# VectorE instead of GpSimd widens the reciprocals of the softmax sums

## The reference

```python
attn = jax.nn.softmax(scores, axis=-1)
out = jnp.einsum('bhcqk,bhckd->bhcqd', attn, vcat)
```

## Time and profile before

| | before |
|---|---|
| median of 3 runs | 3150.91 us (3148.77 to 3153.44) |
| the profiled execution | 3158.34 us |
| its span, first to last instruction | 3156.5 us |
| mean granted TensorE clock | 0.948 |
| PE busy | 2776.2 us |
| DVE busy | 2502.5 us |
| ACT busy | 2397.7 us |
| POOL busy | 2640.5 us, 1590 instructions |
| instructions, all engines | 54604 |

### The profile page before, as it was taken

How to read it: one execution, slowest core, us unless ns; L and a number is a source line. 1 busy time by engine, 2 the same in 40 slices (tenths; PEclk the granted TensorE clock), 3 DMA queues, 4 the chain that set the end, 5 groups by cost and what they waited for, 6 DMA issues and landing times.

```text
span 3156.5 us, 54604 instructions
## 1 busy us (share of the span) xinstructions
PE 2776.2 (88%) x17328; PEld 1765.1 (56%) x17328; DVE 2502.5 (79%) x5644; ACT 2397.7 (76%) x5299; POOL 2640.5 (84%) x1590
## 2 busy tenths in 40 slices
PE   4788788899999999999899899999999899978657
PEld 3555445465565656566565656656565655654326
DVE  3256988889797978889797988979788897989970
ACT  4677878888796978878797888879798787965432
POOL 1116999999998999999999999999899989988870
PEclk9899999999999999999999999999999999999778
DMA  3005353545445454644545464544646454465541
GB/s 84 14 11 168 124 170 98 194 146 186 146 147 195 142 195 144 220 136 138 179 155 192 129 228 144 158 160 145 209 126 214 142 180 152 147 195 189 175 125 42
DMA packets 285967, 477.31 MB, mean 151 GB/s; under 512 B 38451, under 2 KB 93363, under 8 KB 285683
## 3 DMA queue, kind: packets, MB, share of 16 engines
q1 hardware_dynamic: 285682, 473.83, 46.0%
HBM read 388.79 MB, written 84.93 MB: 150 GB/s over the span
## 4 chain that ended last, share of the span: by engine, by line
PE 59%; POOL 17%; DVE 9%; issue 8%; ACT 5%; DMA 1%; SPq 1%; DVEq 0%; POOLq 0%; ACTq 0%
PE bank L765 19%; PE bank L773 8%; POOL h_rows L1786 8%; POOL h_rows L1796 7%; PE bank L1024 6%; PE bank L1010 6%; PE bank L963 5%; PE bank L810 4%; PE bank L888 3%; PE bank L798 3%; PE bank L826 3%; DVE h_rows L1562 2%; PE bank L759 2%; DVE prob L1345 2%; ACT prob L1079 1%
## 5 line engine op out<-in xcount | busy, mean ns | idle before, releaser
L1786 POOL TENSOR_TENSOR h_rows<-u_rows,b_rows 128x1024 f32<-128x1024 f32 x512 | 1203.4, 2370 | 23.2 <-DMA b_rows<-bc_dram 19.4
L1796 POOL TENSOR_TENSOR h_rows<-h_rows,c_rows 128x1024 f32<-128x1024 f32 x480 | 1128.5, 2366 | 76.3 <-DVE state L1569 47.0
L1250 ACT ACTIVATE bank<-d_rows,a_rep 128x512 f32<-128x512 f32 x1024 | 682.2, 689 | 222.6 <-DVE v_pad L1372 82.7
L1562 DVE TENSOR_TENSOR_SCAN h_rows<-bank,state,h_rows 128x512 f32<-128x512 f32 x480 | 593.7, 1269 | 47.6 <-ACT bank L1250 42.5
L1562 DVE TENSOR_TENSOR_SCAN h_rows<-bank,h_rows 128x512 f32<-128x512 f32 x480 | 573.0, 1212 | 63.2 <-ACT bank L1250 46.5
L1079 ACT ACTIVATE prob<-prob,neg_max 128x256 f32<-128x256 f32 x1024 | 510.2, 505 | 36.0 <-DVE neg_max L1345 35.9
L1345 DVE CUSTOM_DVE_ANT_0 prob<-bank,bands 128x256 f32<-128x256 f32 x896 | 336.6, 419 | 122.0 <-PE bank L798 75.4
L810 PE MATMUL bank<-ident,prob 128*128 128x128 f32 x2048 | 330.8, 287 | 87.7 <-ACT prob L1079 55.0
L810 PEld LDWEIGHTS bank<-ident,prob 128*128 128x128 f32 x2048 | 237.5, 144 | 273.4 <-issue 140.3
L963 PE MATMUL bank<-h_rows,sum_n 128*32 128x512 f32 x2048 | 298.0, 662 | 74.3 <-POOL h_rows L1796 55.9
L1010 PE MATMUL bank<-y4T,w 128*128 128x256 f32 x1024 | 250.9, 392 | 12.7 <-DMA e_b<-in_b 10.8
(11 more groups left out here) (164 smaller groups left out, 4852.9 us busy)
## 6 DMA issues: line engine op xcount, KB each, us to landing
u_rows<-u_dram SPq DMA_DIRECT2D x256, 256.0 KB, 3.9
d_rows<-delta_dram SPq DMA_DIRECT2D x256, 256.0 KB, 4.1
b_rows<-bc_dram SPq DMA_DIRECT2D x256, 256.0 KB, 3.1
c_rows<-bc_dram SPq DMA_DIRECT2D x256, 256.0 KB, 3.2
w<-in_W SPq DMA_DIRECT2D x28, 1024.0 KB, 6.8
zs_dram<-region_b SPq DMA_DIRECT2D x64, 256.0 KB, 3.7
xc_dram<-region_b SPq DMA_DIRECT2D x64, 256.0 KB, 2.7
u_dram<-region_b SPq DMA_DIRECT2D x64, 256.0 KB, 5.0
```

The source lines that it names most:

```text
L1250: e.activation(banks[at.bank][:, :], d_rows[:, c, :], ACT.Exp, scale=a_rep[:, k:k + 1]).then_inc(filled[at.bank], 1)
L1562: e.tensor_tensor_scan(rows, banks[at.bank][:, :], rows, start, ALU.mult, ALU.add).then_inc(drained[at.bank], 1)
L1786: e.tensor_tensor(half_of(i, b, half), u_rows[:, 2 * half:2 * half + 2, :], twice(b_rows[:, b % 2, :]), ALU.mult).then_inc(bx_ready.sem, 1)
L1796: e.tensor_tensor(rows, rows, twice(c_rows[:, b % 2, :]), ALU.mult).then_inc(hc_ready.sem, 1)
```

## The change

`widen` moves, word for word, from GpSimd's part of the attention to VectorE's, at the same beat (8w + 11) of the same stage, behind `reciprocals` of the beat before. All numbers of `PLACES`, `THREADS` and `LEADS` are replaced too.

The order that the new numbers give is close to the old one, and not the same. Leaving out `widen` and the empty pieces, VectorE has 2528 pieces; 1897 of their 2527 pairs of neighbours stay neighbours, and no piece moves by more than 8 places. On TensorE it is 1596 of 1831 pairs and 4 places, on ScalarE 1884 of 2878 and 13, on SP's queue 705 of 956 and 8, on GpSimd (with the old place of `widen` kept in the count) 1103 of 1431 and 4. Nearly all of it is one piece of a scan changing places with one piece of another stage beside it. The numbers of the banks differ for most tiles, as they are handed out along the way. The list of ScalarE's functions has 81 changes of table before and after.

On VectorE, `widen` stands right behind `reciprocals` in the windows 1, 3, 4, 5 and 6 of a group in the even part. In the windows 0, 2 and 7 one to three pieces of other stages stand between them (scans, and pieces of the rwkv and middle stages).

```diff
@@ PLACES, THREADS, LEADS: every number replaced, as here
     "attention": (
-        1154, 1246, 1506, 1592, 1696, 1696, 1985, 1985, 2053, 2179, 2244, 2252, 2406, 2454, 2475, 2486, 2495, 2496,
+        1168, 1225, 1458, 1685, 1760, 1920, 2146, 2146, 2146, 2213, 2246, 2246, 2399, 2466, 2481, 2554, 2554, 2554,
...
@@ dve_attention
                     e.wait_ge(*rden_wide_ready.at(i, w - 1))
                 e.reciprocal(rden[:, heads], den[:, c % 2, heads]).then_inc(rden_ready.sem, 1)
 
+            def widen(w):
+                k = w % 2
+                e.wait_ge(*rden_ready.at(i, w + 1))
+                if w > 1:
+                    e.wait_ge(*full(use(f"a{w - 2}")))
+                e.tensor_copy(rden_wide[:, k * P:(k + 1) * P].rearrange("p (h d) -> p h d", d=HD),
+                              rden[:, 8 * k:8 * k + 8].rearrange("p (h o) -> p h o", o=1).broadcast_to([P, 8, HD])
+                              ).then_inc(rden_wide_ready.sem, 1)
+
...
                 if beat % 8 == 2 and beat >= 10 and beat < 72:
                     reciprocals((beat - 10) // 8)
+                if beat % 8 == 3 and beat >= 11:
+                    widen((beat - 11) // 8)
                 yield
@@ pool_attention
-            def widen(w):
-                k = w % 2
-                e.wait_ge(*rden_ready.at(i, w + 1))
-                if w > 1:
-                    e.wait_ge(*full(use(f"a{w - 2}")))
-                e.tensor_copy(rden_wide[:, k * P:(k + 1) * P].rearrange("p (h d) -> p h d", d=HD),
-                              rden[:, 8 * k:8 * k + 8].rearrange("p (h o) -> p h o", o=1).broadcast_to([P, 8, HD])
-                              ).then_inc(rden_wide_ready.sem, 1)
-
...
             for beat in range(AFTER - ATT0):
-                if beat % 8 == 3 and beat >= 11:
-                    widen((beat - 11) // 8)
                 if beat % 8 == 7 and beat >= 15:
```

More of the change, by code:

```diff
@@ L51 @@
     "head": (
-        -1295, -228, -174, 428, 922, 922,
+        -1622, -446, -340, 345, 925, 1156,
     ),
     "attention": (
[6 rows of a table removed]
[6 rows of a table added]
     ),
     "mlp": (
-        8488, 9615, 10328, 10408, 10582, 10582, 10679, 10679, 10862, 10863, 10931, 11191, 11195, 11370, 11370, 11427,
-        11754, 12216, 12231, 12421, 12563, 12813, 12894, 12941, 13050, 13050, 13254, 13314, 13400, 13617,
+        7523, 9595, 10531, 10585, 10622, 10630, 10636, 10636, 10809, 10954, 10954, 11035, 11076, 11264, 11328, 11519,
+        11933, 12203, 12256, 12400, 12610, 12843, 12945, 12995, 13097, 13097, 13294, 13314, 13577, 13617,
     ),
     "rwkv": (
-        14273, 14533, 14534, 14534, 14630, 14717, 14961, 15098, 15171, 15422, 15422, 15496, 15696, 15946, 15978,
-        16191, 16232, 16438, 16546, 16684,
+        14227, 14502, 14503, 14526, 14598, 14667, 14961, 15024, 15189, 15422, 15422, 15528, 15658, 15966, 15997,
+        16227, 16251, 16539, 16539, 16690,
     ),
     "middle": (
-        16764, 16935, 17333, 17392, 17511, 17571, 17650, 17824, 18009, 18084, 18109, 18270, 18298, 18339, 18339,
-        18437, 18459, 18771, 18772, 18772, 18820, 18855, 19035, 19035, 19114, 19608, 19859, 19924, 19936,
+        16792, 16922, 17251, 17377, 17511, 17571, 17650, 17825, 18007, 18064, 18097, 18298, 18298, 18298, 18313,
+        18413, 18516, 18771, 18772, 18878, 18878, 19027, 19176, 19253, 19294, 19843, 19844, 19864, 19990,
     ),
     "scan": (
[10 rows of a table removed]
[10 rows of a table added]
     ),
     "back": (
-        30607, 31803, 31982, 32248, 32346, 32497, 32584, 32830, 33037, 33300,
+        30341, 31789, 31790, 32271, 32380, 32587, 32746, 32833, 33038, 33298,
     ),
     "route": (
-        33454, 33801, 33972,
+        33403, 33805, 33885,
     ),
     "fetch": (
-        43666,
+        43460,
     ),
     "expert": (
-        44497, 44581, 45065, 45317, 45317, 45705, 45845, 46037, 46078, 46628, 46723, 46881, 47060, 47556, 47655,
-        47943, 47960, 48079, 48238, 48825, 48926, 49093, 49247, 49247, 49733,
+        44480, 44590, 45030, 45294, 45294, 45677, 45838, 46035, 46171, 46702, 46718, 46855, 47034, 47521, 47655,
+        47899, 47946, 48074, 48082, 48771, 48885, 49013, 49241, 49241, 49852,
     ),
@@ L103 @@
 THREADS = (
[L104 to L110, removed]
+    (("head", "attention",), (-3974, -1637, -1878, -1870, -1843, -1868, -1867, -1885, -1885, -1885, -1880, -1894, -1879, -1910, -1895, -1945)),
+    (("mlp", "rwkv", "middle",), (-1651, -1880, -1865, -1845, -1870, -1870, -1894, -1887, -1887, -1881, -1881, -1896, -1894, -1889, -1938, -2018)),
+    (("scan",), (-1895, -1834, -1840, -1862, -1868, -1872, -1863, -1885, -1885, -1873, -1870, -1900, -1887, -1923, -1988, -1472)),
+    (("back",), (-1837, -2394, -2397, -1869, -1867, -1832, -1866, -2324, -1884, -1879, -1813, -1858, -2062, -2104, -1875, 313)),
+    (("route",), (1155, -1746, -4346, -1889, -3024, -1590, -1913, -2076, -1979, -1976, -2720, -1774, -1790, -1961, 1979, -289)),
+    (("fetch",), (-2607, -2351, -2014, -2042, -1482, -1852, -2404, -1657, -929, -1904, -1933, -1440, -2236, 713, 997, 5025)),
+    (("expert",), (-1821, -1853, -1867, -1875, -1873, -1873, -1941, -1876, -1884, -1885, -1889, -1952, -2008, -3026, 6197, 8482)),
 )
@@ L117 @@
         "head": (
-            -19, 0, 108, 317, 21, 121,
+            72, 476, 86, 107, -128, -292,
         ),
         "attention": (
[4 rows of a table removed]
[4 rows of a table added]
         ),
         "mlp": (
-            -361, -32, -368, -463, -298, -66, -66, -129, -273, -481, 0, 0, 0, 0, 186, -93, -1, 205, -34, -614, -731,
-            0, -4, -99, -4, -191, 0, 63, -25, -184,
+            -191, -32, -273, -380, -495, -51, -25, 61, -220, -8, 252, -212, 165, -147, 202, -87, -25, 148, 144, -677,
+            -1170, -59, -251, -136, -184, -125, 174, 522, 538, -59,
         ),
         "rwkv": (
-            -4, -31, 235, 169, -539, 233, 0, 29, 55, -126, -27, -425, -23, 0, -684, -333, -358, -493, -358, -358,
+            -1, 42, -59, 40, -83, -89, 7, 74, -93, 0, 0, -38, -38, -38, 0, -80, -88, -49, -2, 0,
         ),
         "middle": (
-            -24, -24, -103, 161, -84, -679, 27, -164, -148, -66, -18, -352, -31, -49, -244, 69, -205, -186, -218, 0,
-            -473, -435, 68, -162, -153, -187, -76, -114, -658,
+            8, -259, -95, 122, -77, -515, 27, -304, -191, -252, -61, -268, 0, -399, -157, 48, -79, -224, -391, -360,
+            -678, -714, 11, -259, -29, -253, 97, -167, -301,
         ),
         "scan": (
[7 rows of a table removed]
[7 rows of a table added]
         ),
         "back": (
-            -1056, 83, -46, -1, -62, 118, -89, -262, 149, 211,
+            -550, 86, 76, -13, 253, -244, -64, -251, 99, 437,
         ),
         "route": (
-            355, -227, -66,
+            -28, 5, 27,
         ),
         "fetch": (
-            -473,
+            -255,
         ),
         "expert": (
-            0, 22, -14, -198, 0, -602, -4, 139, 74, -6, -75, 0, 0, 0, 0, 0, 0, 71, -81, 102, 131, -595, 3, 0, 0,
+            0, 158, 0, -233, 21, -625, -4, 403, -152, 58, 54, 0, 0, 0, 0, 0, 0, -317, -460, 125, 41, 457, 211, 226,
+            0,
         ),
@@ L160 @@
         "head": (
-            20, 74, 215, 285, 51, 51,
+            217, 430, 576, 0, 0, 0,
         ),
         "attention": (
[5 rows of a table removed]
[5 rows of a table added]
         ),
         "mlp": (
-            621, 381, -184, 187, -467, -365, -890, -900, -688, -592, -451, -129, -156, 0, -68, 0, 228, 248, 248, 248,
-            0, 0, 0, 0, -7, 0, 16, 0, 0, 543,
+            234, 232, -263, 0, -285, -169, -9, 188, -77, -526, 0, 0, 0, 0, 0, 210, 0, 0, 0, 0, 0, 0, 0, 0, 0, 0, 0,
+            0, -327, 493,
         ),
         "rwkv": (
-            -101, -155, -26, -176, 18, -235, -42, -42, 0, 379, 571, 314, 14, -74, 6, -44, -1, -19, -207, 0,
+            151, -63, 14, -169, 0, -279, -167, -331, 44, 266, 15, 192, 66, 15, -41, 0, 80, -356, -220, 38,
         ),
         "middle": (
-            0, 279, 0, 0, 84, 172, 0, -41, -133, -599, 14, 80, 0, 0, -125, -177, 82, -48, 75, -121, 180, -17, 352, 0,
-            -346, -808, 260, -445, 0,
+            167, 412, -27, 116, 84, 172, 70, 0, -133, 0, 14, 57, -22, -149, -22, -280, 4, -51, 67, -66, -8, 0, 183,
+            42, -955, -901, 258, 0, 0,
         ),
         "scan": (
[7 rows of a table removed]
[7 rows of a table added]
         ),
         "back": (
-            -76, 232, -106, 30, 18, -1020, 139, 170, 170, 68,
+            -295, 166, -133, -210, 11, -1368, -11, 624, 800, -590,
         ),
         "route": (
-            0, -187, 0,
+            178, 136, -448,
         ),
         "fetch": (
-            174,
+            834,
         ),
         "expert": (
-            -199, -276, 0, 0, 0, -44, -283, 91, 104, 91, -307, -27, -160, 11, 41, -47, -695, -18, -210, -210, 110,
-            67, 93, 299, 909,
+            577, 141, -2, -332, -659, 322, 717, 341, -9, 23, 1, 24, 0, -61, 696, 595, 335, 0, 611, -167, 94, 212, 96,
+            300, -438,
         ),
@@ L205 @@
```

(64 more changed lines are left out.)

## The result

The changed kernel takes 3285.85 us (median of 4 runs, 3283.39 to 3295.55) against 3152.18 for the kernel before on the same chip. The ratio is 1.0425, with a 95% interval of 1.0404 to 1.0445. That is 134 us slower, where 58 were forecast, and above the end of the range, 3272. The profiled execution took 3295.55 us.

The account below looks back on a forecast made before the run. No engine alone was the bound: TensorE, GpSimd and VectorE are full together in the attention windows. Relief 0, copies' wait +58, reordering 0 gave +58 us on 3150.91, so 3209 us, range 3157 to 3240 (0.54); if slower, 3165 to 3272.

Parts of the forecast that it names:

- The size of the copies: 128 copies on VectorE: 0.23 us alone, 1.25 with the wait for GpSimd's multiplications, 130 us in 13 groups.
- The choice between the two rows: VectorE's copy waits for GpSimd like the router's tensor_scalar (2277 ns once), not like the reciprocals (never above 203 ns).
- How much reaches the end: Share of VectorE's added 130 us that reaches the kernel's end: 45%, the middle of two bounds, so 58 us.
- Rival C: All of VectorE's delay is passed on: 73%, 95 us, or 115 with a worse order; 3246 to 3266; chance 0.22.
- The lower bound: In the attention windows VectorE's 7.27 us of idle time absorbs all but 1.48 of 8.75 us of copies: 17%.
- GpSimd's relief: Copies leaving GpSimd free 4.0 us a group, 52 us over 13 groups; taken as 0 in the forecast.
- Rival A: Copies under 1.04 us let GpSimd's relief win: up to 52 us, 3116; chance 0.17 with Rival D's better half.
- The reordering costed at nothing: New order of the engines' lists: nearly all one piece past its neighbour, 0 us, but it widens the range.
- that bound of 59: GpSimd's wait for VectorE in `times_c`: the order can give or take up to 59 us over the even part.
- Rival D: Steps do not all keep their place; order alone decides, within 59 us of 3151; better half within Rival A's 0.17.

Follow-up runs that it names:

- the number put back: Changed kernel with one number of ScalarE's `LEADS`, for the expert stage's first piece, back from -595 to 82: 3242.99 us, ratio 1.0285.
- even work: Old order, `widen` on VectorE as a reduce, each followed by a useless reduce over 768 constants: 3222.98 us against 3152.39, ratio 1.0229.

## Why the prediction was wrong

**The size of the copies: right, with some luck.** The prediction had 0.23 us alone and 1.25 with the wait, 130 us in the 13 groups of the even part. Measured were 130.5 us in the same groups (141.6 in all), and some 0.23 us for each copy of the first two groups, where GpSimd hardly ran beside it. The mean of 1.25 came out in part by luck: two copies that waited for four multiplications each, 8.7 and 8.6 us, are 17 us of the 130.5, while the prediction had bounded a wait by one multiplication; the other 102 have 1.11 on average, and the median of the 104 is 1.10, not 1.2. With the copies alone, in the old order, the same groups had 143.0 us. The choice between the two rows was the right one: the copy waits as the tensor_scalar of the earlier trace rows did, not like the reciprocal. One of them in the changed kernel, VectorE and then GpSimd (timeline):

```profile
1096.31 0.62 DVE L1362 COPY rden_wide<-rden 128x128 f32<-128x128 f32 x1
```

```profile
1094.48 2.37 POOL L1783 TENSOR_TENSOR h_rows<-u_rows,b_rows 128x1024 f32<-128x1024 f32 x1
1096.79 4.72 POOL L1793 TENSOR_TENSOR h_rows<-h_rows,c_rows 128x1024 f32<-128x1024 f32 x2
```

The copy starts in the middle of a multiplication and ends at 1096.93, 0.08 us behind its end.

**How much reaches the end: too low.** The step took the middle of 17% and 73%, 45%. With the old order, where this can be read by itself, the copies cost 89 us, 58% of their 154.1 and 72% of what they take beyond the reduce. Rival C, 73% passed on, had 95 us for this. The lower bound was wrong as a guide: that all idle time of the windows can be used is nearly true for the first half microsecond of a copy (29% passed on), and not for what lies above it.

**GpSimd's relief: right at 0, as far as it was seen.** Rival A needed copies that cost under 1.04 us. The reduce costs 0.286, and still nothing comes back. GpSimd was busy for 82.34 of 84 us in the windows; with the reduce on VectorE it is busy for 79.03 of the same 84, and the time is the same. It has less to do and waits longer. This is the relief less the reduce's own 36.6 us on VectorE: no kernel took `widen` from GpSimd and gave VectorE nothing, so the worth of the relief by itself stays open.

**The reordering costed at nothing: the step that failed.** It reads "nearly all of it is one piece past its neighbour", and it bounded the cost by GpSimd's waits. It costs 62 us, as it happens near that bound of 59, but by another way: one piece of ScalarE's, the longest move of all (the 13 places were on record), and a piece that does nothing but wait for a DMA. Such a piece is not worth its own time, which is 0, but the time until what it waits for arrives. ScalarE then holds exp for the first window, TensorE its next scores, and VectorE its masks. For loads the prediction looked at GpSimd's waits only. Rival D had the right thought, that the steps do not keep their places, but took its price from GpSimd's waits as well. With the copies alone the time is 3242, inside the range up to 3272; this one piece took it out.

Together: 58 forecast; 89 for the copies and 62 for the one piece, less 17 that overlap, are 134.

## What to carry to other kernels

Before an SBUF-to-SBUF copy goes to VectorE beside a GpSimd that is always multiplying, look for a form that does not wait: a reduce over one element did the same work in 0.286 us, and two copies of odd counts did it in 0.43 us together, where the plain copy took 1.2 us on average. When an order written out by numbers changes, do not count the places that moved: look for the pieces that hold only a wait, and ask for each when what it waits for arrives. An engine that looks full may give nothing back when it is relieved: here GpSimd's 4 us a group bought no time, although VectorE had to take only 0.286 us a window for them.

## What was not expected of the hardware

A copy does not wait for one multiplication at most. The longest in the changed kernel, VectorE and then GpSimd (timeline):

```profile
894.13 8.69 DVE L1362 COPY rden_wide<-rden 128x128 f32<-128x128 f32 x1
```

```profile
893.46 4.69 POOL L1793 TENSOR_TENSOR h_rows<-h_rows,c_rows 128x1024 f32<-128x1024 f32 x2
898.08 4.66 POOL L1783 TENSOR_TENSOR h_rows<-u_rows,b_rows 128x1024 f32<-128x1024 f32 x2
```

It started in the first of four multiplications that followed each other without a gap, and ended at 902.82, with the last. At three ends the next one of GpSimd came first. In the changed kernel 2 of 128 copies waited through more than one multiplication (with the number put back it was four, of 3.6 to 9.2 us); the others ended with the multiplication that they met, or with one that began as they did. The Trainium skill, "SBUF — State Buffer", section "Who interferes with whom", says that whoever comes second is blocked for the other's whole instruction: that agrees for the rest, and these two waited for four. What decides who comes first at such an end stays open. So does why the waiting copies cost more than even work: that the long ones reach TensorE (it waited 6.5 us for the copy at 894 in the same stretch) was seen, but no run had the waits made even.

A reciprocal of 128 elements takes 947 ns and one of 8 takes 197, so (947 - 197) / 120 = 6.3 ns for an element, and none of the 128 waited for GpSimd.
